# Gate weights by tanh inside the up phase of their own step, and x of the next step turned ahead of the first probabilities

## What is computed

```python
scores = xt @ gate_w
ew, ei = jax.lax.top_k(scores, K)          # K = 2
ew = jax.nn.softmax(ew, axis=-1)
mask = ei[None, :, :] == jnp.arange(E)[:, None, None]
wE = jnp.sum(ew[None, :, :] * mask, axis=-1)
...
y = _layernorm(xt[None, :, :] + o, ln_g[:, None, :], ln_b[:, None, :])
out = jnp.einsum('et,etd->td', wE, y)
```

## Time and profile before

| | |
|---|---|
| median of 3 runs | 270.11 us (268.58 to 270.12) |
| profiled execution | 268.45 us |
| its span, first to last instruction | 266.7 us |
| PE busy | 235.2 us, 88% |
| DVE busy | 183.2 us, 69% |
| ACT busy | 159.4 us, 60% |
| POOL busy | 134.7 us, 51% |
| mean granted clock of PE | 0.976 |

### The profile page before, as it was taken

The page is one execution under the profiler, slowest core; times in us unless marked ns, Lnnn a source line. Parts: engine busy times, 40 slices in busy tenths (PEclk is TensorE's granted clock), DMA queues, the critical chain, the costliest instruction groups (busy, mean ns, idle before and its releaser), DMA issues.

```text
span 266.7 us, 7792 instructions
## 1 busy us (share of the span) xinstructions
PE 235.2 (88%) x3064; PEld 201.8 (76%) x3064; DVE 183.2 (69%) x570; ACT 159.4 (60%) x419; POOL 134.7 (51%) x254
## 2 busy tenths in 40 slices
PE   7796889998999999999999899998999999989970
PEld 3455468887888888888888788887888888858960
DVE  2989858485866677686967587677858595455175
ACT  2454408836695648744893759654884479356650
POOL 8082655247713674266714771367525660378075
PEclk9996899999999999999999999999999999999995
DMA  7930000000000000000000000000000000000000
GB/s 199 366 140 2 2 2 0 2 4 4 0 20 6 0 2 20 4 2 4 20 2 2 0 2 21 5 2 2 20 2 2 2 21 2 4 0 0 22 0 21
DMA packets 5652, 6.23 MB, mean 23 GB/s; under 512 B 336, under 2 KB 5104, under 8 KB 5360
## 3 DMA queue, kind: packets, MB, share of 16 engines
q1 hardware_dynamic: 5616, 5.74, 6.7%
HBM read 4.68 MB, written 1.05 MB: 21 GB/s over the span
## 4 chain that ended last, share of the span: by engine, by line
PE 47%; DVE 24%; ACT 16%; POOL 7%; issue 5%; POOLq 0%; ACTq 0%; DVEq 0%
ACT hid L484 11%; PE z L1003 6%; PE turns L867 6%; PE score L974 6%; DVE q_st L590 6%; PE score L966 5%; ACT L445 3%; DVE ypart L660 3%; PE turns L869 3%; PE turns L868 3%; DVE xn L570 3%; PE score L985 3%; PE score L1048 2%; POOL rstd L340 2%; ACT prob L445 2%
## 5 line engine op out<-in xcount | busy, mean ns | idle before, releaser
L484 ACT ACTIVATE hid<-turns,pack_ffn 128x256 f32<-128x256 f32 x128 | 50.4, 472 | 39.3 <-PE turns L869 39.3
L1003 PEld LDWEIGHTS z<-w,hid 128*128 128x128 f32 x480 | 59.4, 191 | 3.7 <-issue 1.0
L1003 PE MATMUL z<-w,hid 128*128 128x128 f32 x480 | 61.5, 276 | 0.0
L309 POOL TENSOR_SCALAR zvar<-zss 128x4 f32<-128x4 f32 x32 | 6.2, 193 | 78.4 <-DVE zss L646 69.4
L323 POOL TENSOR_TENSOR ypart<-ypart 128x256 f32<-128x256 f32 (+1 forms) x60 | 36.0, 600 | 18.4 <-DVE ypart L660 15.4
L867 PE MATMUL turns<-h_hi,w_hi 128*128 128x256 f32 x128 | 39.7, 310 | 5.0 <-ACT hid L484 4.8
L868 PE MATMUL turns<-h_lo,w_hi 128*128 128x256 f32 x128 | 35.9, 280 | 0.0
L869 PE MATMUL turns<-h_hi,w_lo 128*128 128x256 f32 x128 | 35.9, 280 | 0.0
L660 DVE SCALAR_TENSOR_TENSOR ypart<-z,zcoef,ln_gG 128x128 f32<-128x128 f32 x120 | 34.1, 341 | 1.8 <-POOL zcoef L314 1.7
L310 POOL TENSOR_TENSOR zrstd<-zvar,mhalf 128x4 f32<-128x4 f32 x32 | 33.1, 1033 | 2.7
L867 PEld LDWEIGHTS turns<-h_hi,w_hi 128*128 128x128 f32 x128 | 24.0, 188 | 9.8 <-ACT hid L484 9.5
(11 more groups left out here) (143 smaller groups left out, 454.7 us busy)
## 6 DMA issues: line engine op xcount, KB each, us to landing
w<-in_w SPq DMA_DIRECT2D x2, 1024.0 KB, 7.2
out_x<-yout SPq DMA_DIRECT2D x8, 128.0 KB, 1.8
x_tokens<-in_x SPq DMA_DIRECT2D x1, 896.0 KB, 6.7
ln_g<-in_ln_g SPq DMA_DIRECT2D x1, 512.0 KB
pack_mod<-in_pack_mod SPq DMA_DIRECT2D x1, 385.0 KB, 3.0
pack_proj<-in_pack_proj SPq DMA_DIRECT2D x1, 193.0 KB, 4.3
pack_att<-in_pack_att SPq DMA_DIRECT2D x1, 130.5 KB, 4.2
x_tokens<-in_x SPq DMA_DIRECT2D x1, 128.0 KB, 2.9
```

Source lines behind the costliest of these rows:

```text
L484: last = a.activation(hid[:, e, c, :], U[(e + 1) % 2][:, c * STEP:(c + 1) * STEP], ACT.Gelu, bias=b1[:, e, c:c + 1])
L1003: last = mm(z_bank(f, q)[:, e * D:(e + 1) * D], hid[:, ee, c, tt * P:(tt + 1) * P], w2[:, ee * CH + c, :], start=False, stop=e == HALF - 1 ...
```

## The change

- The two weights are written with tanh: of the difference d of the two scores they are 0.5 - 0.5 tanh(d/2) and 0.5 + 0.5 tanh(d/2), which is the softmax of two. ACT computes `gtanh` in the up phase of the same step, behind the third expert's gelu; `exp_weight` is gone from the start of a body and from the last one.
- On DVE `weights(i)` stands in the up phase of step i, behind the last scale and ahead of the statistics, and waits for `gtanh`. The one-hot rows are one compare and one product over 128x32 in place of four instructions. `weights_T(i)` comes behind the statistics, `add_ln_b(i)` between the second and the third shift. A body on DVE then begins with `normed_front(n)`.
- On PE `turn_weights(i)` stands behind the fifth up and `ln_b_sum(i)` behind the seventh (in step 7 behind the seventh and the eighth), in the bank `zB[1]` (in step 7 `S[1]`) in place of `U[1]`. `down(f, 1)` waits for `lnb_out`; `proj_k` and `turn_x2` do not any more.
- On PE `turn_x(n)` stands between `down(f, 0)` and `turn(i, 0)` for i from 1 to 6.

```diff
             def weights(f):
 
-                dve.wait_ge(gexp_s, f + 1)
-                cf.link(v.tensor_scalar(gden[:, :], gexp[:, :], 1.0, None, ALU.add))
-                cf.link(v.reciprocal(gw[:, :, 0], gden[:, :]))
-                cf.link(v.tensor_tensor(gw[:, :, 1], gexp[:, :], gw[:, :, 0], ALU.mult))
-                for tt in range(TILES):
-                    for j in range(2):
-                        last = v.tensor_scalar(wsel[:, tt, j, :], iota[:, :], gidf[:, tt, j:j + 1],
-                                               gw[:, tt, j:j + 1], ALU.is_equal, ALU.mult)
-                cf.link(last)
+                dve.wait_ge(gtanh_s, f + 1)
+                cf.link(v.tensor_tensor(chosen[:, :, :, :], bc(bc(iota[:, :], 1, 2), 1, TILES),
+                                        bc(gidf[:, :, :], 3, EXPERTS), ALU.is_equal))
+                v.tensor_scalar(gw[:, :, 0], gtanh[:, :], -0.5, 0.5, ALU.mult, ALU.add)
+                cf.link(v.tensor_scalar(gw[:, :, 1], gtanh[:, :], 0.5, 0.5, ALU.mult, ALU.add))
+                cf.link(v.tensor_tensor(wsel[:, :, :, :], chosen[:, :, :, :], bc(gw[:, :, :], 3, EXPERTS), ALU.mult))
...
                     gelu(i, 2)
+                    tanh_weight(i)
                     gelu(i, 3)
...
             def turn_weights(f):
                 pe.wait_ge(wexp_s, f + 1)
-                pe.wait_ge(gelu_s, 8 * f + 7)
+                if f == STEPS - 1:
+                    pe.wait_ge(x1_s, f + 1)
+                elif f > 0:
+                    pe.wait_ge(u_done, 4 * f)
+                else:
+                    pe.wait_ge(bias_o_s, 1)
...
                 if i == 0:
                     keep_warm(8)
+                if nxt and i > 0:
+                    turn_x(n)
                 if att:
                     turn(i, 0)
```

More of the change, by code:

```diff
@@ L194, in z_bank, with weight_bank @@
             return S[q] if f == STEPS - 1 and q > 1 else zB[q % 2]
+        def weight_bank(i):
+            return S[1] if i == STEPS - 1 else zB[1]
         def here(n):
@@ L457, in square, with tanh_weight @@
                 a.activation(zsq[:, q % 2, :], z_bank(f, q)[:, :], ACT.Square).then_inc(sq_s, 1)
-            def exp_weight(f):
-                act.wait_ge(gdif_s, f + 1)
-                a.activation(gexp[:, :], gdif[:, :], ACT.Exp).then_inc(gexp_s, 1)
+            def tanh_weight(i):
+                act.wait_ge(gdif_s, i + 1)
+                a.activation(gtanh[:, :], gdif[:, :], ACT.Tanh, scale=0.5).then_inc(gtanh_s, 1)
             def square_sum(f, q):
@@ L633, in weights_T @@
                     dve.wait_ge(pad_s, 1)
-                v.tensor_copy(wexpT[0:EXPERTS, :], U[1][0:EXPERTS, 0:STEP]).then_inc(wT_out, 1)
+                v.tensor_copy(wexpT[0:EXPERTS, :], weight_bank(f)[0:EXPERTS, 0:STEP]).then_inc(wT_out, 1)
             def add_ln_b(f):
@@ L812, in body @@
                 n, f = i + 1, i - 1
[L813 to L816, removed]
                 if nxt and i > 0:
@@ L819, in body @@
                 if ffn and att:
-                    add_ln_b(f)
+                    zsum(f, 0)
+                if ffn and att:
                     scale(f, 0)
@@ L842, in body @@
                     scale(f, 3)
+                if att:
+                    weights(i)
                 if i + 2 < STEPS:
                     stats_front(n + 1)
+                if att:
+                    weights_T(i)
                 if nxt:
-                    for s in range(GROUPS):
-                        shift(n, s)
+                    shift(n, 0)
+                    shift(n, 1)
+                if att:
+                    add_ln_b(i)
+                if nxt:
+                    shift(n, 2)
+                    shift(n, 3)
                 if i == STEPS:
-                    weights(f)
-                    weights_T(f)
                     scale(f, 0)
                     scale(f, 1)
-                    add_ln_b(f)
                     scale(f, 2)
@@ L1015, in down_start @@
                 pe.wait_ge(gelu_s, 8 * f + HALF * (half + 1))
+                if f < STEPS - 1 and q == 1:
+                    pe.wait_ge(lnb_out, f + 1)
                 if f == STEPS - 1 and q > 1:
@@ L1029, in turn_weights @@
                 pe.wait_ge(wexp_s, f + 1)
-                pe.wait_ge(gelu_s, 8 * f + 7)
+                if f == STEPS - 1:
[4 more added lines that the diff above has]
+                    pe.wait_ge(bias_o_s, 1)
                 for tt in range(TILES):
-                    last = tr(U[1][0:EXPERTS, tt * P:(tt + 1) * P], wexp[:, tt, :], ident[:, :])
+                    last = tr(weight_bank(f)[0:EXPERTS, tt * P:(tt + 1) * P], wexp[:, tt, :], ident[:, :])
                 last.then_inc(wT_done, 1)
@@ L1039, in ln_b_sum @@
                 for tt in range(TILES):
-                    last = mm(U[1][:, STEP + tt * D:STEP + (tt + 1) * D], wexpT[:, tt * P:(tt + 1) * P], ln_bG[:, f // PER_BATCH, :],
+                    last = mm(weight_bank(f)[:, STEP + tt * D:STEP + (tt + 1) * D], wexpT[:, tt * P:(tt + 1) * P], ln_bG[:, f // PER_BATCH, :],
                               start=True, stop=True)
@@ L1115, in body @@
                     down(f, 1, 1)
-                if nxt:
+                if nxt and i == 0:
                     turn_x(n)
-                if ffn:
-                    ln_b_sum(f)
                 if att:
@@ L1159, in body @@
                     up(i, 4)
+                    if i < STEPS - 1:
+                        turn_weights(i)
                 if att:
@@ L1165, in body @@
                     up(i, 6)
+                    if i == STEPS - 1:
+                        turn_weights(i)
+                    else:
+                        ln_b_sum(i)
                 if i == STEPS - 1:
```

22 lines of the change are left out of this document (7 added, 15 removed).

## The result

The changed kernel takes 279.98 us (median of 5 runs, 277.8 to 280.51), the kernel before 270.11: a ratio of 1.036, with a 95% interval from 1.0314 to 1.0406. It is 9.9 us slower where the forecast said 5.5 (275.6, and a range of 272.0 to 281.0). The profiled execution took 277.8 us with a span of 276.0, against 268.45 and 266.7: 9.3 us more of span. Executions of one kernel spread over some 2 us (the kernel before: 268.3 to 270.3 in 19 runs), and in the profiles the spread lies ahead of the first gelu, which starts at 39.4 to 39.7 us where the profiled execution was one of the shorter ones of its kernel and at 40.7 to 41.2 where it was one of the longer ones. The direction, the place and the mechanism were as forecast; the size was not, and the difference has a cause of its own, which I had left out.

The account below looks back on a forecast made before the run. The prediction took PE's run from the first turned probabilities to the q projection as the bound. Six steps +6.2, last body -0.9 and tail +0.5 gave +5.8 us, forecast as 275.6 us, range 272.0 to 281.0.

Parts of the forecast that it names:

- What bounds the kernel: PE runs without a gap from the first turned probabilities to the q projection's end, 7.83 us; that end moves the step.
- Part 1: PE between first probabilities and q: weight turns, turn of x and ln_b sum leave, so 7.83 us shrinks to 6.94.
- Part 3: PE's early turn of x waits for DVE's xn: 1.7 us idle, 1.04 us longer a step, +6.2 us in six.
- Part 2: Up phase: DVE idles some 1.1 us for tanh, weights take 0.83; first shift 2.32 us later, first exp 0.4.
- My bounds: Range of the lengthening per step from xn's wait, with DVE's small operations shorter or longer: 0.7 to 1.6 us.
- Part 4: Last steps: body 7 gains 0.86 us as DVE's first scale starts earlier; the tail loses 0.45 and 0.05 us.
- The sum: Whole kernel: six steps +6.2, last body -0.9, tail +0.5, together +5.8 us; forecast 275.6 us.
- The clock: Rival: PE's clock falls to half in the 1.7 us idle; 278.3 us with one fall, 283.7 with three; chance 0.14.
- load of a table: Rival: two table loads a step on ACT around the tanh, 20.5 us in eight steps, 296 us; chance 0.02.
- DVE is there in time: Rival: xn comes early enough for the turn of x to fit PE's hole; -3.3 us, 266.8 us; chance 0.06.

Follow-up runs that it names:

- xn in the middle: Changed kernel with DVE writing the next x's xn between the ln_b add and the third shift, x still turned first: 270.12 us, ratio 1.0013.
- the run with both: Changed kernel with xn written between ln_b add and third shift, and POOL waiting for wexp before its last add of experts: 267.06 us, ratio 0.9914.

## Why the prediction was right, and where its size was off

*What bounds the kernel, and Part 1.* Right. The PE stretch from the turn of x to q shrank as reckoned, 7.20 us against 7.16. With x back at its old place the kernel is 2.5 us above the one before from the first gelu on, with xn in the middle 1.0 us.

*Part 3, the wait for xn.* Right in place and mechanism. PE idles 1.6 us in front of the turn of x (forecast 1.7), six times, released by DVE's xn. That the 1.6 came so near to the 1.7 is partly luck: both of its ends were later than forecast by nearly the same (in the step shown PE is free at t = 9.88 and not 9.31, xn there at 11.50 and not 11.00), both through the weights. DVE idles 0.91 us in front of the compare (forecast about 1.1).

*Part 2, the weights on DVE: the term that was mis-sized.* I had 0.83 us from the compare to the statistics, and gave each small operation the duration that the rows of before showed. There they had run beside an idle POOL. In their new place they run beside POOL's adds of experts, and take 1.23 to 1.39. Where POOL is out of the way they take just the 0.83: in body 0 (compare at 43.06, statistics at 43.88), and in all steps of the run in which POOL waits. My bounds (0.7 to 1.6 us a step) did hold the 1.4 that came, but for another reason than the one that made them. The second half of the same error is on PE: turning the weights started at t = 4.24 to 4.39 and not at 3.83, so the up phase grew by 0.8 to 1.0 us and not by 0.4. In the steps with an x to turn this is hidden behind the wait for xn; in step 7 it is not.

*Part 4.* The gain of the last step was forecast at 0.86 and came at 0.26 (27.78 to 27.52); with POOL waiting it is 0.81. The tail grew by 0.66, forecast 0.5.

*The sum.* In the profiled executions: six periods +8.76 us (forecast 6.2), step 7 -0.26 (forecast -0.9), the tail +0.66 (0.5), the start +0.14: 9.3 together. Of the 3.4 or so that were missed, 2.3 are POOL in the five periods between the steps 1 and 6 (152.51 us against 150.26 with POOL waiting), 0.55 are POOL again in step 7, and 0.55 are the first period; the tail and the start give 0.3, and the five periods without POOL would have been 0.3 shorter than forecast. That first period is 30.66 with and without the waiting POOL, where gdif stands 2.74 us beside POOL's product; its cure was tried and only moved the standstill, so for this part the cause is read from the trace and not shown by a run.

*The rivals.* The clock did not fall: it is full (1.00) through all steps, with holes of 1.6 us in six of them. No load of a table stands beside the tanh: the next gelu starts 0.10 us behind it, and the loads are two a step as before. The Trainium skill, "ScalarE: Activation LUTs", section "Table sets: the hidden batching unit", lists gelu's set without tanh; the trace does not bear that out. "DVE is there in time" was priced at 3.3 us below before, from xn early enough and nothing else in the way. That is what the run with both is; it came at 2.8 below by the medians, 2.3 by the trace.

## What to carry to other kernels

An instruction moved ahead of others in an in-order queue brings its wait with it: look up when its input is written on the other engine, and what the same change has put in front of that. A duration read from the trace holds for the neighbours that it had there; if an operation of DVE is moved beside work of POOL, price it with POOL's instruction in front of it. And where a change loses, try its parts in other places before dropping it: this one lost 3.6%, and gains about 1% with one pair of instructions moved and one wait added.

## What the runs showed of the hardware

- A 128x2 operation on DVE (0.15 to 0.17 us by itself) can take 0.47 us beside POOL's adds of 128x256 and 2.74 us beside POOL's product of 128x1024: its end follows the end of POOL's instruction by 0.02 to 0.04 us. Statistics and shifts beside the same work of POOL kept their lengths. A wait added to POOL made the kernel 2.8 us faster from the first gelu on.
- Holes of 1.6 us on PE, one in each of six steps, left its clock at the full level (1.00), and so did one of 1.68 us in body 0; in the hole of 2.22 us of body 0 in the kernel before, and right behind one of 3.76 us in body 0 of the changed kernel, it went to half.
- A tanh between gelus needed no load of a table (0.20 us, and 0.10 from its start to the next gelu).
